# A graph kernel's pass over the attention's peaks: ScalarE derives the mask of absent members from the one-hot, in place of a second compare on VectorE

## What is computed

```
xt        = (x @ W.T + bias).reshape(n, H, C)            # H = 4 heads of 32
alpha_src = sum(xt * a_src, -1);  alpha_dst = sum(xt * a_dst, -1)
alpha     = leaky_relu(alpha_src[row] + alpha_dst[col], 0.2)
amax      = segment_max(alpha, col)                       # the peaks
ex        = exp(alpha - amax[col])
out       = segment_sum(xt[row] * ex / segment_sum(ex, col)[col], col)
```

## Time and profile before

| | us |
|---|---|
| median of the runs | 13578.29 |
| the profiled execution's own time | 13585.59 |
| its span, first to last instruction | 13583.8 |
| the pass of the peaks, about | 4472 to 5602 |

### The profile page before, as it was taken

The page is one execution under the profiler, slowest core; times in us unless marked ns, Lnnn a source line. Parts: engine busy times, 40 slices in busy tenths (PEclk is TensorE's granted clock), DMA queues, the critical chain, the costliest instruction groups (busy, mean ns, idle before and its releaser), DMA issues.

```text
span 13583.8 us, 192267 instructions
## 1 busy us (share of the span) xinstructions
PE 10090.9 (74%) x68184; PEld 8162.2 (60%) x68289; DVE 7971.0 (59%) x13503; ACT 3712.1 (27%) x6670; POOL 6409.9 (47%) x6626
## 2 busy tenths in 40 slices
PE   6796067758665788764689868986998699899444
PEld 3675067657654333454688768876887688644333
DVE  8754066436444888777688646764676477600334
ACT  0242040220313577532332033203320332154000
POOL 0277776777773677300045603460455045501776
PEclk8665599989988999998999999999999999999555
DMA  1000087556663333322799768876887688776222
GB/s 54 2 4 18 16 269 227 177 182 190 207 194 107 110 106 107 88 81 81 248 310 314 203 214 281 294 203 215 287 287 204 215 294 272 244 297 254 53 53 56
DMA packets 1073032, 2382.23 MB, mean 175 GB/s; under 512 B 199212, under 2 KB 385888, under 8 KB 1045028
## 3 DMA queue, kind: packets, MB, share of 16 engines
q0 software_dynamic: 354208, 926.60, 25.0%
q10 hardware_dynamic: 403392, 811.55, 17.0%
q1 hardware_dynamic: 314564, 632.22, 13.1%
HBM read 1211.29 MB, written 1158.47 MB: 174 GB/s over the span
## 4 chain that ended last, share of the span: by engine, by line
PE 39%; POOL 26%; issue 15%; DVE 11%; DMA 7%; ACT 1%; DVEq 1%; ACTq 0%; POOLq 0%; SPq 0%
PE ps L2024 15%; PE ps L2044 14%; POOL list L739 6%; POOL list_f L739 6%; POOL rows_work L760 6%; POOL rows_work L771 5%; PE ps L2134 5%; POOL rows_work L795 3%; DMA rows_work<-messages_R,rows_R 2%; DVE rows_work L1507 2%; DMA rows_work<-near 2%; DMA rows_work<-messages_F,rows_R 2%; PE ps L1957 1%; PE ps L2036 1%; DMA ADM<-near 1%
## 5 line engine op out<-in xcount | busy, mean ns | idle before, releaser
L2024 PE MATMUL ps<-H,onehot 128*128 x23760 | 3191.4, 286 | 1038.2 <-DVE rows_work L1507 535.3
L795 POOL DMA_INDIRECT rows_work<-messages_F,rows_R x1890 | 1828.1, 967 | 4038.5 <-DMA messages_F<-rows_work 2640.3
L2024 PEld LDWEIGHTS ps<-H,onehot 128*128 128x128 f32 x23760 | 2905.3, 196 | 1243.9 <-issue 1174.4
L2044 PE MATMUL ps<-rows_work,onehot 128*128 128x128 f32 (+1 forms) x15840 | 2157.0, 282 | 329.6 <-DMA rows_work<-messages_F,rows_R 193.1
L932 ACT CAST onehot<-rows_work 128x512 f32<-128x512 uint8 x1980 | 1222.5, 618 | 3818.9 <-PE ps L2024 2515.0
L2044 PEld LDWEIGHTS ps<-rows_work,onehot 128*128 128x128 f32 x15840 | 1951.6, 192 | 496.8 <-issue 446.8
L1507 DVE TENSOR_TENSOR rows_work<-ps,list_words 128x512 f32<-128x512 f32 x2160 | 1484.4, 688 | 847.3 <-PE ps L2024 847.0
L1515 DVE TENSOR_TENSOR onehot<-ps,list_words 128x512 f32<-128x512 f32 x1980 | 1355.7, 688 | 599.4 <-PE ps L2044 581.3
L760 POOL DMA_INDIRECT rows_work<-rel_table,rows_F x832 | 788.0, 947 | 967.6 <-DMA rel_table<-list_words 714.4
L739 POOL DMA_INDIRECT list<-list_words,rows_R x831 | 812.9, 978 | 849.3 <-DVE rows_R L1273 576.2
L795 POOL DMA_INDIRECT rows_work<-messages_R,rows_R x1080 | 1021.1, 946 | 388.0 <-issue 261.7
(11 more groups left out here) (350 smaller groups left out, 10981.2 us busy)
## 6 DMA issues: line engine op xcount, KB each, us to landing
messages_F<-rows_work ACTq DMA_DIRECT2D x630, 792.0 KB
messages_R<-rows_work ACTq DMA_DIRECT2D x360, 792.0 KB
rel_table<-list_words SPq DMA_DIRECT2D x196, 1024.0 KB, 3.8
rows_work<-onet SPq DMA_DIRECT2D x480, 192.0 KB
gat_rows<-rows_work SPq DMA_DIRECT2D x220, 264.0 KB, 2.1
rows_work<-gat_rows SPq DMA_DIRECT2D x220, 264.0 KB, 2.7
ADM<-onet SPq DMA_DIRECT2D x240, 192.0 KB
rows_work<-near SPq DMA_DIRECT2D x180, 192.0 KB
```

Source lines behind the costliest of these rows:

```text
L795: pool.indirect_dma_start(out=ring2[:, G2 % RING2, :], out_offset=None, in_=rows_dram[PASSES[r]], in_offset=bass.IndirectOffsetOnAxis(ap=t ...
L2024: ins = mm(ps[:, G1 % 3, j * P:(j + 1) * P], onet_f[G1 % 2][:, j * P:(j + 1) * P], hflat[:, bass.ds(at["blocks"][g % GPW], FEAT)], start=T ...
L2044: ins = mm(into, member, ring2[:, G2 % RING2, j * AUX:j * AUX + width], start=False, stop=True, skip_group_check=True)
```

## The change

ScalarE makes `absent` as the activation Identity of the one-hot with scale -1 and bias 1 (a new constant column `ones_1`), 128x512, bfloat16 out, ahead of the quad's 12 small instructions. It waits for the one-hot (`peak_members`). VectorE's compare L1646 is gone, so the small maxima called by `between(0)` and `between(1)` stand one behind the other. `peak_members` is raised twice a quad, `diag_ready` five times; TensorE waits for ScalarE ahead of L2079. A memset of one column is added ahead of the pass.

```diff
@@ scratch
+        ones_1 = sb("ones_1", [P, 1])
@@ peak_pass, ScalarE
                     if q >= 2:
                         act.wait_ge(peak_summed, q - 1)
+                    act.wait_ge(peak_members, 2 * q + 1)
+                    slots = slice(q % 2 * QUAD, (q % 2 + 1) * QUAD)
+                    nc.scalar.activation(absent[:, slots, :], onehot[:, slots, :], ACT.Identity, bias=ones_1[:, 0:1], scale=-1.0).then_inc(diag_ready, 1)
@@ VectorE, ahead of the pass
-            st(v.memset(ADM[:, :, HEADS:], -BIG))
+            st(v.memset(ADM[:, :, HEADS:], -BIG), False)
+            st(v.memset(ones_1[:, :], 1.0))
@@ peak_operands, VectorE
                 v.tensor_tensor(onehot[:, slots, :], numbers, node, ALU.is_equal).then_inc(peak_members, 1)
                 between(0)
-                v.tensor_tensor(absent[:, slots, :], numbers, node, ALU.not_equal).then_inc(peak_members, 1)
                 between(1)
@@ TensorE
-                pe.wait_ge(peak_members, 3 * q + 2)
+                pe.wait_ge(diag_ready, (QUAD + 1) * q + 1)
...
-                pe.wait_ge(peak_members, 3 * q + 3)
+                pe.wait_ge(peak_members, 2 * q + 2)
                 for t in range(q * QUAD, (q + 1) * QUAD):
-                    pe.wait_ge(diag_ready, t + 1)
+                    pe.wait_ge(diag_ready, t + q + 2)
```

## The result

Thirteen runs of each kernel: 13627.63 us after (13599.59 to 13645.51), 13586.72 us before (13573.32 to 13624.82). The ratio of the changed kernel to the one before is 1.0023, with a 95% interval of 1.0013 to 1.0034: slower by 31 us, 18 to 46 (the ratio goes by the means, which lie 31.7 us apart; the medians lie 41 apart). The change took 150 us of work from VectorE and lost 31.

What follows compares the result with a forecast made beforehand. GpSimd's gathers, 5.13 us a quad, bound the kernel. Third gathers held by the diagonals add 31 us, all else 0: 13585.6 becomes 13617, and 13610 as the runs' median lies 7 below the profiled one; range 13560 to 13657.

Steps and rivals of the forecast that it cites:

- meeting point: Where a quad's third gather starts against VectorE's instructions; moving it 0.02 us either way makes +31 us +18 or +48.
- GpSimd sets the pace: Four gathers make the quad's 5.13 us and VectorE waits for them, so taking 0.68 us off VectorE gains nothing.
- A gather that starts inside a two-input instruction is held: A gather starting inside VectorE's compare L1646 waits till 0.56 us after the compare's start, then takes its 0.94.
- L1653 at 1.14 after the copy: The fourth head's diagonals on VectorE start 1.14 us after the copy L1007 (L1011 after the change).
- 0.57 caught for 0.49 us: About 57 in 100 third gathers are held by the diagonals, 0.49 us each: 0.28 us a quad against 0.138.
- The border: Start offset inside L1365, in the last stage, up to which gathers are free: 0.043 us; held from 0.045 on.
- The other gathers stay free: A quad's first, second and fourth gathers meet no hold after the change, so only the third is stretched.
- All caught: Rival, chance 0.22: without a gap between VectorE's instructions over nine in ten third gathers are held, +60 to +77 us.
- None caught: Rival, chance 0.09: the second small maximum starts 0.04 us later, most third gathers pass ahead of the diagonals, -30 us.
- ScalarE and TensorE at no cost: ScalarE's 0.62 us mask fits the quad and TensorE's mask matmuls still start at + 1.5: cost 0.
- pair: What VectorE's back-to-back two-input instructions would hand on; without a gap, over nine in ten third gathers are held.
- A gather ahead of it costs VectorE up to 0.08 us: A third gather starting ahead of the fourth head's diagonals costs VectorE up to 0.08 us, which it has.

Runs made afterwards that it cites:

- e3: Changed kernel, with VectorE also making the second compare at its old place into unread words, ScalarE still making the mask: ratio to the kernel before 1.0003, pass 1128.8 us.
- e1: Changed kernel, with the fourth head's diagonals (L1653) moved ahead of the second small maximum: ratio to the kernel before 0.9998, pass 1129.9 us.
- e2: Changed kernel, with the fourth head's diagonals (L1653) moved behind the third small maximum: ratio to the kernel before 0.9974, pass 1106.9 us.
- e8: Changed kernel, with the fourth head's diagonals made by four one-input tensor_scalar instructions instead of one tensor_tensor: ratio to the kernel before 0.9982, pass 1099.2 us.
- e6: Kernel before, with VectorE's mask L1646 made from the one-hot by a one-input tensor_scalar: ratio to the kernel before 0.9979, pass 1100.0 us.
- e7: Changed kernel, with a memset of 128 columns added between the second small maximum and L1653: ratio to the kernel before 1.0012, pass 1140.2 us.
- e4: Changed kernel, with a memset of one column added between the second small maximum and L1653: ratio to the kernel before 1.0009, pass 1140.0 us.
- e5b: Changed kernel, with ScalarE's mask cut to one of 128 columns from the third quad on: ratio to the kernel before 1.0021, pass 1152.7 us.

## Why the prediction was right

The forecast was +31 us; the ratio gives +31 (18 to 46) and the pass +29.7. The absolute 13610 lies 18 us under the median of 13627.6: 8 are the kernel before's own median, 13586.7 here against the 13578.3 that the forecast started from, and 10 that the medians lie 41 apart. That the difference came out within 2 us is in part luck: by the forecast's own reckoning 0.02 us in the meeting point is worth 16 us, and two sizes below were off.

- *GpSimd sets the pace.* Right: VectorE lost 0.68 us a quad, and its wait for gathered rows grew from 0.35 to 0.75; e3 gives the work back at no cost.
- *A gather that starts inside a two-input instruction is held.* Right, and now shown by intervention: e1 and e3 move the meeting point to the tail (pass 1129.9 and 1128.8), e2 moves it away, e8 takes the second input away (1106.9 and 1099.2). But two inputs are not the whole condition, which the forecast did not need: a fast instruction with one holds as well (e6, L1436).
- *L1653 at 1.14 after the copy.* Right: median 1.145 us. *0.57 caught for 0.49 us.* 0.54 for 0.49. Two errors lie in it and nearly cancel, by luck. The border was taken from L1365, which starts on an idle VectorE, as 0.044 us; here, behind the small maximum, it is 0.030, which alone would make 0.62. But about one quad in eight has a late landing, which the forecast did not have, and there the third gather falls somewhere else: 0.29 of those 28 are caught, and 0.58 of the other 184.
- *The other gathers stay free.* Nearly: in quads with a late landing some fourth gathers are held too, 1.3 us in all.
- *All caught*, the rival on the slower side, rested on the hold passing from one two-input instruction to the next without a gap where they lie back to back. The border is indeed earlier there, by 0.014 us and not by the 0.07 it needed. *None caught* would have needed L1653 0.05 later than it came.
- *ScalarE and TensorE at no cost.* Right in the sum, wrong in two sizes. The mask takes 0.72 us and not 0.62, and starts 0.88 after L1011 (5597.14 against 5596.26) and not 0.82, so the matmuls on the mask start at + 1.66, not + 1.5, and TensorE then waits for the diagonals, which the forecast had 0.15 us early each: 3.67 us for its eight matmuls instead of 3.60. It had 0.65 us to give (0.28 left in the quad shown), and VectorE's L1659 never waits for it, so none of this reached the end. A table load takes 1.28 us in the traces; there are four in each of the two, so the change adds none.
- *Who holds whom.* With the meeting place as it was, 0.54 of the third gathers are caught by the one two-input instruction of the changed kernel and none by the four one-input ones of e8. What a gather and such an instruction share, and at which part of its 0.94 us a held gather stands still, no run shows; the "pair" of the prediction and the "port" of the expectations are names for it with nothing measured behind them. L1653 holds from 0.03 to 0.56 of its 0.68 us. *A gather ahead of it costs VectorE up to 0.08 us*: nearly, L1653 takes 0.69 us where the gather starts 0.04 us ahead and up to 0.75 where it starts 0.03 inside and is free, so up to 0.07.

## What to carry to other kernels

Before moving work off an engine, ask what that engine's remaining instructions will meet once they start earlier. In these runs, with indirect DMAs issued by GpSimd at the pace of the stage, each long VectorE instruction with two SBUF inputs (0.63 to 0.69 us) that a gather met was a stretch in which gathers were held, from about 0.03 us after its start (0.04 for L1365, ahead of it in e7) till 0.13 us ahead of its end; so was one with a single SBUF input at the fast pace (e6's mask, till 0.30 of 0.43 us, and L1436, till 0.50 of 0.63). The very short ones did no harm: the small maxima have two SBUF inputs and take 0.16 us, and in the changed kernel all 36 gathers that start within the first 0.08 us of one are free. So count and place the long ones, shorten them, or make them from one input at the ordinary pace (e8), rather than count VectorE's busy time. And where a result hangs on 0.02 us, say so and look for the order that doesn't.

## What the runs showed of the hardware that I had not expected

**Landings came late where an instruction fetch of queue 8 began behind the gather's issue.** Queue 8 ("instruction") moves 22 packets of 16 KB in the pass of every kernel, one in 8 or 12 quads, each taking 0.9 to 1.9 us in the records. In the packet records of the kernel before all 22 begin 0.9 to 1.9 us ahead of the issue of the quad's fourth gather, and the gathered rows are there 2.49 to 2.66 us after that issue. In the changed kernel all 22 begin 0.66 to 1.59 us behind it, and the rows are there after 2.88 to 3.71 us. e2, e4 and e7 have it so in 21 of 22, all late. In e1, e3, e5b, e6 and e8 all 110 begin ahead of the issue, and one landing is late, just so (2.77 us, in e8). The other late quads of the changed kernel (6 of 28) each follow one of these. Queue 14 moves some 62 more packets marked as instructions, of 8 KB and 0.3 to 0.8 us; 11 of them begin 0.6 to 1.6 us behind such an issue in the kernel before, with no late landing. A late quad of the changed kernel, in which VectorE idles 1.13 us and the third gather meets another instruction:

```profile
5005.31 0.17 DVE L1011 TENSOR_SCALAR rows_work<-rows_work 128x16 f32<-128x16 f32 x1 [1.13 <-DMA rows_work<-gat_table,rows_work]
5005.40 0.68 DVE L1649 TENSOR_TENSOR onehot<-iota,list_words 128x512 f32<-128x512 f32 x1
5005.79 1.11 POOL L772 DMA_INDIRECT rows_work<-gat_table,rows_work  x1 [0.30 <-issue]
```

That the fetch is the cause is argued from this coincidence in all kernels, not shown by a run that moved a fetch alone. Which engine fetches, and why the order of VectorE's instructions, or less work on ScalarE (e5b), moves it from one side of the gather to the other, stays open.

**The hold ended 0.12 to 0.13 us ahead of the recorded end of the instruction, at each length met here**: 0.56 of 0.68 us (L1646, L1653), 0.50 of 0.63 (e7's L1654), 0.30 of 0.43 (e6's mask), 0.50 of 0.63 (L1436). Its begin is looser: in e7, where only a short memset lies between the diagonals and the instruction before, gathers that start 0.09 us ahead of their recorded start are held already (hold 0.59 us long instead of 0.53).
